# Dealing the six scan units to two slots in another order, in a fused patch-token, RWKV-style attention and top-2 expert kernel

## What is computed

```
tokens = layernorm(layernorm(patches) @ W1 + b1)            # (8, 64, 64)
h1     = silu(layernorm(concat[tokens, tokens, tokens] @ Wp1 + bp1))
h      = concat[h1 @ Wp2 + bp2, txt]                        # (8, 269, 64)
x      = layernorm(h); delta = shifted(x) - x
r, k, v, w, a, g = projections of x + delta * x_mix[i]      # w, a, g through small two-layer nets
for t:  S = S * exp(w_t) + (S @ -kk_t) b_t^T + v_t k_t^T;  o_t = S @ r_t
h      = h + (groupnorm(o) + (r k r_k) v) * g @ W_o
y      = layernorm(h); the two best of 8 experts by y @ Wg, softmax over the two
h      = h + sum_e combine_e * (relu(y @ W1_e + b1_e) @ W2_e + b2_e)
```

## Time and profile before

| | us |
|---|---|
| median of three runs | 219.96 (219.35 to 220.77) |
| profiled execution | 222.68 |
| its span, first to last instruction | 220.9 |
| TensorE busy in it | 189.3 (86%) |
| VectorE busy | 148.4 (67%) |
| ScalarE busy | 87.2 (39%) |
| GpSimd busy | 74.1 (34%) |
| mean granted TensorE clock | 0.967 |

### The profile page before, as it was taken

How to read it: one execution, slowest core, us unless ns; L and a number is a source line. 1 busy time by engine, 2 the same in 40 slices (tenths; PEclk the granted TensorE clock), 3 DMA queues, 4 the chain that set the end, 5 groups by cost and what they waited for, 6 DMA issues and landing times. The chain is left out here.

```text
span 220.9 us, 3788 instructions
## 1 busy us (share of the span) xinstructions
PE 189.3 (86%) x1259; PEld 144.2 (65%) x1259; DVE 148.4 (67%) x529; ACT 87.2 (39%) x221; POOL 74.1 (34%) x123
## 2 busy tenths in 40 slices
PE   0388663998999999999999999586999879999994
PEld 0374552686867887866967797474957646867662
DVE  2986367737849463957839965968584779786560
ACT  2012421345434445444342242313645444738540
POOL 2802699053725523933635215503000022000000
PEclk9999999999999999999999999965699999999999
DMA  7900000000000000000000000000000000000010
GB/s 213 343 31 1 0 0 0 3 0 3 0 3 1 0 3 0 0 3 0 0 3 1 0 3 0 3 1 0 0 1 11 10 0 12 10 0 18 3 36 18
DMA packets 2354, 4.06 MB, mean 18 GB/s; under 512 B 400, under 2 KB 1552, under 8 KB 2336
## 3 DMA queue, kind: packets, MB, share of 16 engines
q1 hardware_dynamic: 1728, 3.05, 4.1%
q10 hardware_dynamic: 608, 0.77, 1.2%
HBM read 3.24 MB, written 0.59 MB: 17 GB/s over the span
## 5 line engine op out<-in xcount | busy, mean ns | idle before, releaser
L1625 PE MATMUL PS<-XHL,W1h 128*128 128x384 f32 x48 | 19.1, 398 | 0.0
L776 POOL TENSOR_SCALAR ve<-mv 128x6 f32<-128x6 f32 x6 | 1.7, 280 | 51.4 <-DVE mv L1209 51.4
L1637 PE MATMUL PS<-CT,PK 128*128 128x384 f32 x48 | 16.9, 352 | 0.1
L1626 PE MATMUL PS<-XHL,W1l 128*128 128x384 f32 x48 | 17.0, 354 | 0.0
L1160 DVE TENSOR_TENSOR YI<-PS,KC 128x256 f32<-128x256 f32 x24 | 10.1, 420 | 9.6 <-PE PS L1475 9.2
L1475 PE MATMUL PS<-PI,AT 128*128 128x128 f32 x96 | 15.9, 290 | 0.1
L931 ACT ACTIVATE xT<-PS,CL 128x384 f32<-128x384 f32 x24 | 13.1, 580 | 7.0 <-PE PS L1626 6.9
L1491 PE MATMUL PS<-QT,YI 128*128 128x128 f32 x96 | 14.8, 277 | 0.2 <-DVE YI L1160 0.2
L1487 PE MATMUL PS<-YI,QT 128*128 128x128 f32 x72 | 12.2, 292 | 2.9 <-DVE YI L1160 2.9
L876 ACT COPY PI<-PS 128x256 f32<-128x256 f32 x18 | 6.7, 372 | 20.1 <-PE PS L1487 19.8
L931 ACT ACTIVATE FAB<-PS,CL 128x384 f32<-128x384 f32 x24 | 13.1, 579 | 3.4 <-PE PS L1626 3.3
(11 more groups left out here) (216 smaller groups left out, 496.1 us busy)
## 6 DMA issues: line engine op xcount, KB each, us to landing
KC<-in_consts SPq DMA_DIRECT2D x1, 706.0 KB, 6.4
out_h<-H SPq DMA_DIRECT2D x6, 96.0 KB, 1.6
ARCH<-in_w SPq DMA_DIRECT2D x1, 512.0 KB, 9.1
AW<-in_attw SPq DMA_DIRECT2D x1, 484.0 KB, 8.0
PT<-in_patches SPq DMA_DIRECT2D x1, 384.0 KB, 3.7
RW<-in_rows ACTq DMA_DIRECT2D x1, 296.0 KB, 6.9
W<-in_w SPq DMA_DIRECT2D x1, 256.0 KB, 9.2
HT<-in_text ACTq DMA_DIRECT2D x1, 192.0 KB, 4.0
```

What stands on the lines that cost most here:

```text
L1625: mm(z, W1h[:, e * EH:(e + 1) * EH], xhl, start=True, stop=False)
L1626: mm(z, W1l[:, e * EH:(e + 1) * EH], xhl, start=False, stop=True).then_inc(z_ready, 1)
L1637: mm(PS[:, C_BANK[x % 2], 0:HALF * P], PK[:, e * P:(e + 1) * P], gates_of(u), start=True, stop=True).then_inc(c_ready, 1)
```

## The change

Units are dealt ((4, 5), (0, 1), (2, 3)). Both text-only units run in round 0, the image units 0 and 1 in round 1, units 2 and 3 in round 2. The waits for `XT` follow: round 0 waits for the text copies, round 1 for the image copies. The wait on `mv3_ready` goes. The picks are staged in unit 2's row of ARCH, since unit 5's is now written early.

```
-        pickraw = ARCH[0:2 * E, 5, 0:E * P]
+        pickraw = ARCH[0:2 * E, 2, 0:E * P]
...
-        SLOTS = ((4, 0), (1, 2), (3, 5))
+        SLOTS = ((4, 5), (0, 1), (2, 3))
...
                 if r == 0:
                     pe.wait_ge(mix_ready, 1)
                     pe.wait_ge(memsets, 1)
-                    pe.wait_ge(xt_dve, s + 1)
-                    pe.wait_ge(xt_act, s + 1)
+                if r < 2:
+                    pe.wait_ge(xt_dve, r + 1)
+                    pe.wait_ge(xt_act, r + 1)
...
                     if u == 0:
                         pe.wait_ge(l_w2, 16)
-                        pe.wait_ge(mv3_ready, 2)
```

More of the change, by code:

```diff
@@ L383, in run @@
             mixes()
-            clear()
             image(0)
             proj(0, 0)
-            factors()
+            proj(0, 1)
+            lora(0, 0)
+            clear()
             image(1)
-            image(2)
-            lora(0, 0)
-            image(3)
             cum(0, 0)
-            blank()
-            image(4)
             hats(0, 0)
             gates(0, 0)
-            image(5)
+            image(2)
             products(0, 0)
             keep(0, 0)
-            proj(0, 1)
+            lora(0, 1)
             turn(0, 0)
+            factors()
+            lt(0, 0, 0)
             apply(0, 0)
-            lt(0, 0, 0)
-            lora(0, 1)
+            image(3)
+            blank()
+            cum(0, 1)
             tlt(0, 0, 0)
-            cum(0, 1)
             lt(0, 1, 0)
@@ L411, in run @@
             lt(0, 2, 0)
-            proj(1, 0)
+            tlt(0, 2, 0)
+            image(4)
+            lt(0, 3, 0)
             products(0, 1)
             keep(0, 1)
-            tlt(0, 2, 0)
-            lt(0, 3, 0)
-            lora(1, 0)
+            tlt(0, 3, 0)
+            out(0, 0)
             turn(0, 1)
-            tlt(0, 3, 0)
-            cum(1, 0)
+            apply(0, 1)
+            image(5)
             lt(0, 0, 1)
-            out(0, 0)
-            apply(0, 1)
-            hats(1, 0)
             fuse(0, 0)
+            proj(1, 0)
             tlt(0, 0, 1)
             lt(0, 1, 1)
+            lora(1, 0)
+            tlt(0, 1, 1)
+            lt(0, 2, 1)
+            cum(1, 0)
+            tlt(0, 2, 1)
+            lt(0, 3, 1)
+            tlt(0, 3, 1)
+            hats(1, 0)
             gates(1, 0)
+            proj(1, 1)
             products(1, 0)
             keep(1, 0)
-            tlt(0, 1, 1)
-            proj(1, 1)
-            lt(0, 2, 1)
-            apply(1, 0)
[L435 to L441, removed]
+            out(0, 1)
+            lora(1, 1)
+            turn(1, 0)
+            fuse(0, 1)
+            cum(1, 1)
+            lt(1, 0, 0)
+            apply(1, 0)
+            proj(2, 0)
             tlt(1, 0, 0)
-            cum(1, 1)
             lt(1, 1, 0)
-            fuse(0, 1)
             tlt(1, 1, 0)
             hats(1, 1)
-            proj(2, 0)
+            gates(1, 1)
             lt(1, 2, 0)
+            lora(2, 0)
             products(1, 1)
@@ L452, in run @@
             lt(1, 3, 0)
+            remain()
+            keep(1, 1)
+            cum(2, 0)
+            tlt(1, 3, 0)
             turn(1, 1)
-            keep(1, 1)
-            lora(2, 0)
-            tlt(1, 3, 0)
+            out(1, 0)
             lt(1, 0, 1)
-            out(1, 0)
-            gates(1, 1)
-            cum(2, 0)
             apply(1, 1)
             fuse(1, 0)
+            hats(2, 0)
+            gates(2, 0)
             tlt(1, 0, 1)
             lt(1, 1, 1)
+            products(2, 0)
@@ L465, in run @@
+            keep(2, 0)
             tlt(1, 1, 1)
-            hats(2, 0)
-            gates(2, 0)
             proj(2, 1)
             lt(1, 2, 1)
-            products(2, 0)
-            keep(2, 0)
+            apply(2, 0)
             tlt(1, 2, 1)
-            step(1)
-            lt(1, 3, 1)
             turn(2, 0)
             lora(2, 1)
+            lt(1, 3, 1)
             lt(2, 0, 0)
             tlt(1, 3, 1)
+            tlt(2, 0, 0)
+            out(1, 1)
+            lt(2, 1, 0)
             cum(2, 1)
+            tlt(2, 1, 0)
@@ L480, in run @@
+            lt(2, 2, 0)
+            fuse(1, 1)
+            tlt(2, 2, 0)
+            lt(2, 3, 0)
+            tlt(2, 3, 0)
+            hats(2, 1)
+            out(2, 0)
+            step(1)
             read(1)
[L481 to L484, removed]
             gates(2, 1)
-            tlt(2, 0, 0)
-            lt(2, 1, 0)
+            fuse(2, 0)
+            products(2, 1)
             step(2)
-            products(2, 1)
+            keep(2, 1)
@@ L490, in run @@
             read(2)
             stats(0)
-            tlt(2, 1, 0)
+            step(3)
+            apply(2, 1)
+            centre(0)
             turn(2, 1)
[L494 to L498, removed]
+            heads(0)
             read(3)
-            apply(2, 1)
-            heads(0)
-            lt(2, 3, 0)
             lt(2, 0, 1)
+            step(4)
             att(0)
-            tlt(2, 3, 0)
             tlt(2, 0, 1)
-            out(2, 0)
@@ L508, in run @@
-            step(4)
+            read(4)
             lt(2, 1, 1)
-            read(4)
-            tlt(2, 1, 1)
             step(5)
             split(0)
-            fuse(2, 0)
-            remain()
             read(5)
+            stats(1)
+            rest(0)
+            centre(1)
+            tlt(2, 1, 1)
             lt(2, 2, 1)
[L518 to L521, removed]
             feat(0, 0)
             feat(0, 1)
+            tlt(2, 2, 1)
@@ L524, in run @@
+            heads(1)
+            lt(2, 3, 1)
+            att(1)
+            rank(0)
             tlt(2, 3, 1)
[L525 to L528, removed]
+            out(2, 1)
             choose(0)
[L530 to L533, removed]
             split(1)
             rest(1)
+            parts(0)
+            fuse(2, 1)
+            feat(1, 0)
+            weights(0, 0)
+            feat(1, 1)
@@ L536, in run @@
             front(0, 0)
-            feat(1, 0)
             front(0, 1)
-            feat(1, 1)
             front(0, 2)
             rank(1)
+            front(0, 3)
+            back(0, 0)
+            choose(1)
             weights(0, 1)
-            front(0, 3)
-            choose(1)
             parts(1)
-            back(0, 0)
             back(0, 1)
@@ L550, in run @@
             weights(1, 0)
-            front(1, 1)
             weights(1, 1)
@@ L554, in run @@
             step(6)
+            front(1, 1)
+            read(6)
             fold(0)
-            read(6)
+            step(7)
             front(1, 2)
-            step(7)
+            read(7)
             front(1, 3)
-            read(7)
             read(8)
             stats(2)
+            centre(2)
             back(1, 0)
+            back(1, 1)
+            back(1, 2)
             front(2, 0)
-            centre(2)
-            back(1, 1)
+            back(1, 3)
+            heads(2)
             front(2, 1)
-            back(1, 2)
-            heads(2)
+            att(2)
+            back(2, 0)
             front(2, 2)
-            att(2)
-            back(1, 3)
             front(2, 3)
+            split(2)
+            rest(2)
             fold(1)
-            back(2, 0)
-            split(2)
             back(2, 1)
             back(2, 2)
-            rest(2)
             front(3, 0)
@@ L585, in run @@
             rank(2)
+            back(2, 3)
             choose(2)
-            back(2, 3)
             front(3, 3)
@@ L602, in run @@
             back(4, 1)
+            back(4, 2)
             front(5, 0)
-            back(4, 2)
             front(5, 1)
```

## The result

The changed kernel takes 232.41 us (median, 230.29 to 234.83) against 220.06 for the kernel before: a ratio of 1.049 (95% interval 1.043 to 1.055). It is slower by 4.9%, outside the range that was given (214.5 to 227). Its profiled execution took 232.26 us, with a span of 230.5.

A forecast was written before the change was run, and what follows sets the result against it. TensorE was taken as the bound from 38.7 us on. Terms of −1.9, −0.6, +0.7, +6.2, −1.1 and −1.5 gave +1.8, taken as +1.6 on the median of 219.96: 221.6 us, range 214.5 to 227.

The forecast's parts named there:

- Step 1: Round 0, up to fuse(0, 0)'s end: proj(0, 1) starts earlier, needing text only; gain 1.9 us, ending at 59.8.
- Step 2: Rounds from fuse(0, 0)'s end to fuse(2, 0): 55.9 us of priced work plus 8% small waits, 60.4 us; bounds 58.8 and 63.
- Step 3: From fuse(2, 0) to front(0, 0): scan steps and epilogues hang behind fuse(2, 0), 36.6 us; bounds 30 and 41.
- rival (b): Behind fuse(2, 0): the clock falls in the gathered tail, chain products take 4 to 5 us more; median 226, chance 0.2.
- Step 4: The experts, from front(0, 0) to the last sum: 63.7 us instead of 66.3, two feats being done before.
- The conversion: From span to median: the forecast change of +1.6 us was put on the kernel before's median of 219.96, giving 221.6.
- (a): Early stretch: the clock rises at 25 us and stays, gaining 5 us instead of 1.9; median 216.5, chance 0.25.
- (c): Whole kernel: round 0 ends as before, the tail is as narrow as VectorE's sum, both cancel; 219, chance 0.1.

The follow-up runs named there:

- after_mv3: The changed kernel with the wait of back(0, 0) on mv3_ready put back; 230.7 us, ratio 1.038 to the kernel before.
- after_hold: The changed kernel with 53 filler products on TensorE, results unused, from products(2, 1) on to hold the clock in the tail; ratio 1.018 to the kernel before.
- after_images: The changed deal of units with the kernel before's order of calls up to fuse(0, 0), images first; 233.5 us, ratio 1.057 to the kernel before.
- before_gather: The kernel before, its own deal, with scan steps 2 to 5, reads 2 to 4 and most of group 0's epilogue moved behind fuse(2, 0); 235.9 us, ratio 1.064.
- after_warm: The changed kernel with 7 filler products on TensorE, results unused, between 12 and 34 us; 226.4 us, ratio 1.023 to the kernel before.
- after_rank: The changed kernel with tlt(2, 3, 1) moved ahead of rank(0), so ScalarE's QT copy precedes its exponential; ratio 1.040 to the kernel before.
- before_hold: The kernel before with 26 filler products on TensorE, results unused, from lt(2, 2, 1) to fuse(2, 1) in the last round; ratio 0.998.
- before_warm: The kernel before with 14 filler products on TensorE, results unused, between 12 and 38 us; 218.2 us, ratio 0.986.

## Why the prediction was wrong

**Step 1, round 0: right at its end, off on the way.** fuse(0, 0) was to end at 59.8, by the walk at 60.7. It ended at 58.2, and at 60.0 and 60.5 in the two traces of the same calls in which the clock rose later (after_mv3, after_hold). On the way hats(0, 0) came at 27.6 for 32.6 and lt(0, 2, 0) at 46.0 for 48.6, so that the end is off by only 1.6 is in part luck. Two things brought hats(0, 0) forward. This trace has the clock up from 12.0 to 15.4 us and from 18.9 to 25.7, where the walk had it low until 42. And GpSimd's clear was not free before: VectorE's first operation on the tile `mix` took 1.36 us beside it and takes 0.15 now, and proj(0, 0) starts some 1 us earlier for it (16.4 in after_hold and after_mv3, 17.5 in after_images and before_gather, the clock low up to there in all four). after_warm shows that some 5 us more lay in the clock. But the clock did not hold by itself.

**Step 2, the rounds up to fuse(2, 0): small waits undersized.** 60.4 us were forecast, 63.3 measured, 7.4 us over the priced work where 4.5 were taken (TensorE idle for 3.8 of them by the row above). The three places where an lt stands beside its own tlt took 1.32 us each, as named; read(1), which waits for VectorE's sum of step(1), came 1.67 us behind that step's start, for 0.84, and was not. The upper bound of 63 was just passed. fuse(2, 0) began at 121.5 for 120.2.

**Step 3 is the one that failed, by its clock.** It priced the stretch from fuse(2, 0) to front(0, 0) at 36.6 us, all at the high level, with 41 as the bound for the low one, and left the clock to rival (b) with a chance of 0.2. Measured: 42.5. Its walk, place by place, in us from the start of fuse(2, 0):

| | forecast | changed kernel | clock held (after_hold) |
|---|---|---|---|
| step(3) | 7.1 | 6.6 | 7.1 |
| att(0) | 13.6 | 17.0 | 13.7 |
| read(4) | 15.3 | 20.2 | 15.4 |
| step(5) | 17.0 | 21.2 | 17.1 |
| feat(0, 0) | 22.0 | 26.2 | 22.3 |
| att(1) | 26.1 | 30.2 | 26.0 |
| VectorE's queue from att(1) starts | 27.0 | 31.1 | 27.0 |
| its last mask of fuse(2, 1) ends | 37.0 | 42.0 | 37.2 |
| front(0, 0) | 36.6 | 42.5 | 38.3 |

With the clock held the walk is right to 0.3 us at every place up to the last mask. In the changed kernel it is 4.2 us late by step(5) and 4.1 where VectorE's queue starts, all of it lost in the low stage that begins at step(3). That is the term that the forecast put at nothing: what the lower clock costs on the chain. The rest of the 5.9 us: VectorE's queue took 10.8 us for 10.0, and front(0, 0) was put 0.4 ahead of the very mask it was said to need, where it came 0.55 behind it (1.1 in after_hold, which has fillers on TensorE there). The earlier trace rows showed the clock falling in a stretch with TensorE busy for 12.0 of 17.5 us, and the forecast's own sum had it at work for 22.0 of 36.6. So the low clock was not a remote rival; it stood in the step's own numbers.

**Step 4: right.** 63.7 us from front(0, 0) to the last sum were forecast, 64.4 measured.

**The conversion.** The profiled execution of the kernel before was 2.7 us over its median, and I carried that difference over. The changed kernel's profiled execution is 0.15 under its own median. This alone is 2.8 us of the 10.8 by which 221.6 missed. The rest: 1.3 by fuse(2, 0) (2.9 lost in step 2, 1.6 gained on step 1), 5.9 in the stretch, 0.8 behind it.

**The reasoning on what bounds it.** Step 3 called VectorE's queue the limit ("from 27.0 to 37.0 without a break but one"). For the last 11 us the traces bear it out: 10.8 us with one break in the changed kernel, and the same in after_rank with out(2, 1)'s wait gone. For the first 31 us the limit is the chain across the engines, in which TensorE's products count, and so its clock. before_gather shows the cause that the forecast had in the right place and at too low a price: the scan and two groups' epilogues run where too little dense work of other units stands between their links.

**Rivals.** (b) came true, in mechanism and size: the clock fell 6.6 us behind fuse(2, 0) (t = 10 forecast) and cost 4.1 us (4 to 5). Its median of 226 was low for the reasons under step 2 and the conversion. (a) did not happen by itself, since the clock fell again at 25.7; helped by fillers it was worth more than its 5 us (fuse(0, 0) ends at 52.8 in after_warm, 8.9 before the 61.7). (c) did not happen. The Trainium skill, page "TensorE: Matmul & The Clock Gate", section "Why this matters for your kernels", advises against idle gaps between bursts of products in mid-kernel. The direction was borne out (held clock 38.3 us, free clock 42.5), the form was not: the clock fell at 128.1 behind waits of 0.56, 0.75 and 0.83 us, with no long gap.

## What to carry to other kernels

Starting a unit of work earlier earns only what the stage in which it starts had free; where its results are needed last, it can push the dependent chains into one place. Before reordering, ask of each chain what dense work stands between its links afterwards. Here the same chain of some 35 us left 17.6 us exposed behind the fifth unit when threaded through two units' inverses, and 36.0 when gathered. And where the new order leaves TensorE idle for much of a stretch, price its products on the chain at both levels of the clock and let the sum carry the difference; here it was 4.1 us, all in the part of the chain where no other engine's queue was full.

## What the runs showed of the hardware

TensorE's lower level is worth very different amounts in one kernel. Raising it in the image stage took 1.4% off the kernel before, with products whose results nobody reads; in that kernel's last round the same trick brought nothing (0.998), where VectorE was busy for 14.5 of 17.1 us. In the changed kernel it took some 4 us off the tail and 5 off the start.

A row's PEclk is no proof ahead of the trace's first clock record: the kernel before printed 1.00 up to 42.3 us, while its products took 1.89 us for 1.03. In before_hold, which has the same calls up to there, the same stage carries records, and its mean is 0.67:

```profile
9.00:39.05 30.05, 20.00 (x87) 15.06 (x87) 21.32 (x82) 7.69 (x25) 18.49 (x30) 0.67 0.09 31
```

And where the clock rises and falls early on differs from execution to execution: the same calls, without fillers, began fuse(0, 0) anywhere from 54.0 to 58.8 us, and the kernel before's early calls led to proj(0, 1) at 40.72, 39.05 and 40.43.

A GpSimd memset can hold up a small VectorE operation beside it. The first one on the tile `mix` (64x6) took 1.35 or 1.36 us in all six traces in which GpSimd's clear ran at that time, and 0.15 or 0.16 in all eight in which it did not.

The fastest version of this study is before_warm, at 0.986 of the kernel before.
